# Biases of twelve projection tiles through TensorE, their copies on ScalarE, and newly written orders in a two-layer attention and expert kernel

## What is computed

```python
x = L0_attn_x
xn = _layernorm(x, axis=-1)
x = x + _L0_attn_ref(xn, ...) + _L0_ffn_ref(xn, ...)
xn = _layernorm(x, axis=-1)
x = x + _L1_attn_ref(xn, Wq, Wk, Wv) + _L1_ffn_ref(xn, Wg, W1, W2, W3)
```

```python
qg = x @ Wq + bq
Q, gate = (qg[..., :D], qg[..., D:])
K = x @ Wk + bk
V = x @ Wv + bv
...
scores = einsum('bhqd,bhkd->bhqk', rmsnorm(Q, qn_w), rmsnorm(K, kn_w)) / sqrt(HD)
out = einsum('bhqk,bhkd->bhqd', softmax(scores), V) * sigmoid(gate)[..., None]
return out @ Wo + bo
```

## Time and profile before

| | |
|---|---|
| median of 3 runs | 597.06 us (595.44 to 597.9) |
| the profiled execution | 595.26 us, of which the span of the instructions is 593.4 us |
| TensorE busy | 562.4 us (95%), weight loads 312.4 us (53%) |
| VectorE busy | 483.2 us (81%) |
| ScalarE busy | 416.4 us (70%) |
| GpSimd busy | 314.9 us (53%) |
| mean granted TensorE clock | 0.967 of full speed |

### The profile page before, as it was taken

One profiled execution on the slowest core, in us unless ns is written; L12 is line 12 of the kernel. 1 busy time (PEld: TensorE's weight loads), 2 busy tenths in 40 slices (PEclk: granted clock), 3 DMA queues, 4 the chain that ended last, 5 costly groups with the idle time before them and its releaser, 6 DMA issues.

```text
span 593.4 us, 11870 instructions
## 1 busy us (share of the span) xinstructions
PE 562.4 (95%) x3637; PEld 312.4 (53%) x3637; DVE 483.2 (81%) x1075; ACT 416.4 (70%) x824; POOL 314.9 (53%) x432
## 2 busy tenths in 40 slices
PE   7378999999999999999999999999999999999996
PEld 4243245456654555544747746576656557565431
DVE  7998889999989899997869988885774677888652
ACT  2542877986878789776875755668766767657795
POOL 6648754257836554677585443765176253233451
PEclk9865699999999999999999999999999999999999
DMA  8452443464644733466572644655645835633311
GB/s 267 129 213 62 134 128 108 129 191 140 194 148 139 210 116 107 137 198 211 158 223 95 218 125 148 195 156 191 189 147 178 261 111 163 195 93 81 91 50 36
DMA packets 68445, 90.01 MB, mean 152 GB/s; under 512 B 8480, under 2 KB 55328, under 8 KB 67872
## 3 DMA queue, kind: packets, MB, share of 16 engines
q1 hardware_dynamic: 64288, 80.87, 44.4%
q0 software_dynamic: 4096, 8.40, 4.8%
HBM read 66.04 MB, written 22.81 MB: 150 GB/s over the span
## 4 chain that ended last, share of the span: by engine, by line
PE 73%; DVE 13%; POOL 4%; issue 4%; ACT 3%; DMA 1%; POOLq 0%; DVEq 0%; ACTq 0%
PE slot L654 16%; PE slot L669 16%; PE pv_ps L682 16%; PE slot L631 9%; PE slot L644 7%; DVE mx L1107 5%; PE slot L619 2%; PE slot L611 2%; ACT probsT L827 2%; POOL xs_hbm L1201 1%; POOL yg L1212 1%; PE slot L576 1%; PE slot L690 1%; DMA yg<-ys_hbm,index 1%; PE slot L553 1%
## 5 line engine op out<-in xcount | busy, mean ns | idle before, releaser
L1107 DVE TENSOR_REDUCE mx<-slot 128x1 f32<-128x512 f32 x512 | 320.0, 681 | 59.7 <-PE slot L654 58.2
L827 ACT ACTIVATE probsT<-slot 128x512 f32<-128x512 f32 x512 | 272.3, 608 | 61.5 <-PE slot L669 49.3
L654 PE MATMUL slot<-k_stack,q_stack 72*128 72x512 bf16 x512 | 175.1, 395 | 3.0 <-DVE mx L1107 1.8
L669 PE MATMUL slot<-q_stack,k_stack 75*128 75x512 bf16 x512 | 167.0, 384 | 3.6 <-ACT probsT L827 1.3
L682 PE MATMUL pv_ps<-probsT,v 128*32 128x512 f32 x1024 | 118.1, 601 | 0.0
L1224 POOL TENSOR_TENSOR hid<-th,up 128x512 f32<-128x512 f32 (+2 forms) x56 | 71.1, 1274 | 78.4 <-DVE th L964 56.1
L654 PEld LDWEIGHTS slot<-k_stack,q_stack 72*128 72x128 bf16 x512 | 50.6, 100 | 80.0 <-issue 22.3
L669 PEld LDWEIGHTS slot<-q_stack,k_stack 75*128 75x128 bf16 x512 | 49.1, 98 | 66.9 <-issue 12.7
L1212 POOL DMA_INDIRECT yg<-ys_hbm,index x64 | 62.5, 977 | 33.0 <-DVE x L1000 15.8
L1201 POOL DMA_INDIRECT xs_hbm<-xn,index x64 | 64.0, 1000 | 26.4 <-issue 12.9
L631 PE MATMUL slot<-xgT,wbuf 128*128 128x128 f32 (+1 forms) x552 | 67.3, 276 | 0.0
(11 more groups left out here) (143 smaller groups left out, 538.5 us busy)
## 6 DMA issues: line engine op xcount, KB each, us to landing
wbuf<-in_experts SPq DMA_DIRECT2D x46, 544.0 KB, 4.8
q_stack<-parts_hbm SPq DMA_DIRECT2D x32, 288.0 KB
k_stack<-parts_hbm SPq DMA_DIRECT2D x96, 96.0 KB
wbuf<-in_experts SPq DMA_DIRECT2D x62, 128.0 KB, 2.2
xg<-xs_hbm SPq DMA_DIRECT2D x24, 256.0 KB, 3.5
ys_hbm<-ys SPq DMA_DIRECT2D x24, 256.0 KB, 3.8
parts_hbm<-parts SPq DMA_DIRECT2D x14, 384.0 KB
xs_hbm<-probsT SPq DMA_DIRECT2D x2, 2048.0 KB, 8.9
```

The source lines that it names most:

```text
L654: nc.tensor.matmul(ps[:, 0:N], q_stack[0:STACK, h, j * P:(j + 1) * P], k_stack[0:STACK, h, :], start=True, stop=True).then_inc(slot_full, 1)
L669: nc.tensor.matmul(ps[:, 0:N], k_stack[0:STACK + MAXROWS, h, j * P:(j + 1) * P], q_stack[:, h, :], start=True, stop=True).then_inc(slot_fu ...
L827: nc.scalar.activation(probsT[:, k % PROBS, a, :], ps[:, 0:N], ACT.Exp, scale=SCALE).then_inc(slot_free, 1)
L1107: nc.vector.tensor_reduce(mx[:, g, u // J, u % J:u % J + 1], ps[:, 0:N], AXIS.X, ALU.max)\
```

## The change

Three things are changed. For QV of the sequences 1 to 3 PE runs a second product into the same bank, the identity with `bias_tok`, which adds the bias there; ACT, not DVE, then copies the 256 and the 160 columns out. For sequence 0 all stays as it was. MP of the first group, MP(0, 0), is run by DVE. And the orders of all five engines and the banks are new, up to a place where layer 1 begins: from the 515th of 1320 stages on, PE's order is the same as before, and the other engines' orders join the old ones near the same place (ACT's with 489 stages to go, DVE's with 389, POOL's with 113, SP's with 119).

The beginnings of the orders, old (-) and new (+):

```diff
     "PE": """
-XT QV4 SU SG QK2 XT QV4 SG RK SD SU XT M2 QK M2 QK M7 QV M9 NT QV M3 QV M QV M XT E M E4 M2 E M E M E3 M2 E3 M
-E M4 E2 NT M2 PV E2 M E5 M SD M3 E3 QK E2 M2 E2 M2 E M QK M QV M E M QV M2 NT M4 PV M E M E2 M E2 M2 E XG M E
+XT QV4 SU SG XT QK2 QV4 SG SU RK M4 SD M QK M5 QK XT M10 QV NT QV3 M E M E M E2 M3 E XT E2 M3 E4 M E M E M E
+M2 E SD E M3 NT PV E M E3 M E M E QK M E2 M QK M3 QV M E M2 E2 M E M QV M E M E M2 NT E M3 E M PV M E3 M E M2
...
     "ACT": """
-XN XT SH2 XN HI2 XT MI2 SG GS RT SG SU XN SS SU QK HI QK XT HI NT XN XT E14 NT E GS E SS E12 QK E2 QK HI E GS
+XN XT SH2 XN XT HI2 MI SU MI SG QV4 SG RT SS XN SU QK GS QK XT HI QV GS HI NT XN QV2 E2 QV E4 XT E9 NT E SS E8
...
     "DVE": """
-CZ LN XV CS LN QQ QV QQ QV QQ SJ QQ SJ3 NH2 LN QV RE QV RE PT HAND PT QV4 RT GA RW GA SS SL SD NM LN M16 SW QV
-M2 QV M2 QV M12 QV M6 SS M NM M5 SD M2 GS M5 QV2 GS M GS M15 AT M2 QV2 M RT GA M3 SS M GA M6 RW M2 NM GA SL GA
+CZ LN CS XV LN QQ4 QV SJ4 NH QV NH QV LN RE QV RE PT2 HAND GA RT GA RW SS SL NM M16 LN MP SW SD M17 SS SD M4
+NM M5 GS M7 GS2 M23 AT GA M8 RT M SS GA M6 RW M3 GA SL GA NM M6 HAND GA M2 AT M GA M7 SW M2 GA M GA M6 OY M5 SD
...
     "POOL": """
-LN SX4 LN VS SQ BO LN GA SC3 BO SC LN MP PT2 SC BO2 MP SQ SC GA SC2 MP PT MP PT SQ GA MP GA3 SC3 GA MP GA SC
+LN SX4 LN BO VS SQ BO GA LN SC3 PT GA LN SC PT SQ MP SC BO SC3 BO MP2 PT2 SQ MP GA4 SC3 GA MP SC GA SC2 GA SC
...
     "SP": """
-ZERO PW RF2 ZERO WL3 NT RF WL RF WL3 NT PW WL3 RF WL XL WL NT WL XL WL2 XL WL2 NT XL WL XL RF WL6 YS NT RF XL
+ZERO PW RF2 WL ZERO RF WL3 NT WL3 RF WL2 NT PW WL3 RF XL NT XL WL3 RF XL WL NT WL6 XL2 WL2 NT RF WL YS XL PW
...
-PART_OF = {("DVE", "PT"): slice(0, 2), ("POOL", "PT"): slice(2, None), ("DVE", "SS"): slice(1, None),
-           ("ACT", "SS"): slice(1, None), ("DVE", "NM"): slice(1, None), ("ACT", "QK"): slice(2, None)}
+PART_OF = {("DVE", "MP"): slice(0, 1), ("POOL", "MP"): slice(1, None), ("DVE", "PT"): slice(0, 2), ("POOL", "PT"): slice(2, None), ("DVE", "SS"): slice(1, None),
+           ("DVE", "QV"): slice(0, J), ("ACT", "QV"): slice(J, None), ("ACT", "SS"): slice(1, None), ("DVE", "NM"): slice(1, None), ("ACT", "QK"): slice(2, None)}
```

The stages themselves:

```diff
@@ -550,8 +550,11 @@
                     pe.wait_ge(*emptied(("XT", A)))
                     if A == 0 and j == 0:
                         pe.wait_ge(first_in, 48)
-                    nc.tensor.matmul(ps[:, 0:2 * D + VGW[0]], xnT[:, A % 2, j * P:(j + 1) * P], w_tok[:],
-                                     start=True, stop=True).then_inc(slot_full, 1)
+                    last = nc.tensor.matmul(ps[:, 0:2 * D + VGW[0]], xnT[:, A % 2, j * P:(j + 1) * P], w_tok[:],
+                                            start=True, stop=(A == 0))
+                    if A >= 1:
+                        last = nc.tensor.matmul(ps[:, 0:2 * D + VGW[0]], ident[:], bias_tok[:], start=False, stop=True)
+                    last.then_inc(slot_full, 1)
                 elif kind == "VG":
                     A, half = stage[1:]
                     pe.wait_ge(*emptied(("XT", A)))
@@ -726,6 +729,12 @@
                     A = stage[1]
                     sc.wait_ge(*filled(stage))
                     nc.scalar.activation(xnT[:, A % 2, :], ps[:, 0:N], ACT.Copy).then_inc(slot_free, 1)
+                elif kind == "QV":
+                    A, j = stage[1:]
+                    sc.wait_ge(*filled(stage))
+                    nc.scalar.activation(qk_tok[:, 2 * j * D:2 * (j + 1) * D], ps[:, 0:2 * D], ACT.Copy)
+                    nc.scalar.activation(vgl[:, J * seq(A) + j, :], ps[:, 2 * D:2 * D + VGW[0]], ACT.Copy)\
+                        .then_inc(slot_free, 1)
                 elif kind == "QK":
                     A, a = stage[1:]
                     sc.wait_ge(*filled(stage))
@@ -896,12 +905,7 @@
                                             bias_tok[:, 0:2 * D], ALU.add).then_inc(qq_done, 1)
                 elif kind == "QV":
                     A, j = stage[1:]
-                    if A == 0:
-                        ve.wait_ge(qq_done, j + 1)
-                    else:
-                        ve.wait_ge(*filled(stage))
-                        nc.vector.tensor_tensor(qk_tok[:, 2 * j * D:2 * (j + 1) * D], ps[:, 0:2 * D],
-                                                bias_tok[:, 0:2 * D], ALU.add)
+                    ve.wait_ge(qq_done, j + 1)
                     nc.vector.tensor_tensor(vgl[:, J * seq(A) + j, :], ps[:, 2 * D:2 * D + VGW[0]],
                                             bias_tok[:, 2 * D:2 * D + VGW[0]], ALU.add).then_inc(slot_free, 1)
                 elif kind == "VG":
@@ -1106,6 +1110,16 @@
                     ve.wait_ge(*filled(stage))
                     nc.vector.tensor_reduce(mx[:, g, u // J, u % J:u % J + 1], ps[:, 0:N], AXIS.X, ALU.max)\
                         .then_inc(slot_free, 1)
+                elif kind == "MP":
+                    A, g = stage[1:]
+                    for u in range(HG * J):
+                        ve.wait_ge(*emptied(("M", A, g, u)))
+                    hi, mid, lo = (mx_parts[:, g, a] for a in range(MAXROWS))
+                    link(nc.vector.tensor_scalar(mx_neg[:], mx[:, g], -1.0, None, ALU.mult))
+                    link(nc.vector.tensor_copy(hi, mx_neg[:]))
+                    link(nc.vector.tensor_tensor(mx_rest[:], mx_neg[:], hi, ALU.subtract))
+                    link(nc.vector.tensor_copy(mid, mx_rest[:]))
+                    nc.vector.tensor_tensor(lo, mx_rest[:], mid, ALU.subtract).then_inc(mxp_done, 1)
                 elif kind == "AT":
                     A, f = stage[1:]
                     ve.wait_ge(*filled(stage))
```

More of the change, by code:

```diff
@@ new lines @@
+SG M RK E2 M DN E M GU E XG E PV E2 M2 E GU E M2 E QK E M XG M SG E QK M E AT E M SU XG DN M E M2 OT M E2 M2
+E2 M GU E NT M3 GU M PV E5 M XG M2 DN M E2 M OY E M2 E2 M DN M2 SD M E2 M NT M2 E M E GU E M3 DN M XG E SD E
+M2 E M E2 M GU M2 E M2 PV E M E2 M2 NT E DN M3 E2 M XG M E DN E M3 E M E M GU E M3 E M E PV E M E NT M2 E2 M E
+M E M E DN M E2 M2 E2 XG M E M2 GU E M2 E XG M E M E M AT E2 GU E2 M E PV M E M2 E M DN XG M E NT XG E M E M3
+E2 AT M E GU E PV E M2 E2 OT M DN M E2 M E2 M OY M2 E XT E M E3 M3 E QK M E M NT E GU M E VG M PV E VG E M E M
@@ new lines @@
+DN E M DN M2 E AT NT XT E QK E3 M2 VG2 M E XG M E2 M E GU M E2 M2 E M PV E M E2 RK XG E M E2 QK E M GU E M3 E
+QK M DN M E2 XG M2 NT E M2 E M DN M E2 M4 GU M2 E PV M E M E M E2 NT E M E M E M2 DN E M E2 M E2 M AT M2 E3 M
+E PV E M E M2 E2 M OT M E2 M E2 M NT OY M E3 M E2 M E2 M E PV M E3 M2 XG M E M E M E2 GG E UU E GG E NT GG E M
+UU M UU E M E M E M AT E M2 E DN E2 XG M E4 PV M XT M E3 M3 E3 M QK E M E2 M E M2 PV GG AT NT UU M GG2 UU2 M2
+OT E2 M2 OY DN M E2 M E M E2 M VG M2 E M QK M XT VG M E M2 E3 VG E M XG M E2 M NT VG M2 E M4 GG2 UU GG UU2 PV
@@ new lines @@
+QK GS QK HI QV E4 QV E2 NT E2 PO E6 XG2 HI E QV NT E6 GU E QV E5 XG E GU E2 RT SS E3 SU NT E DN E2 SG E3 DN E
+GU XG E3 PO E3 GU XG E QK E3 QK SG SU GS XG E DN OT E4 NT E GU2 E4 HI DN E3 XG E3 DN E NT E3 GU E DN E XG E4
+GU E HI E PO E NT E DN E4 XG DN E4 GU E3 NT E8 DN XG E5 XG E GU E3 GU E4 PO E DN XG E NT E4 GU E2 XN E2 XG OT
+DN E6 XT E6 NT E2 QK GU PO E XN E DN E DN E2 XT NT E3 QK HI E XG E4 RT E GU E HI E5 XG E2 QK E GU E QK E DN E
+XG NT E3 DN E2 GU E PO E3 NT E8 DN E9 OT E2 NT E13 XG E3 GG E PO E3 UU GG E UU GG UU NT E5 HI E DN E2 XG E2 XN
@@ new lines @@
+E XT E9 HI E PO QK NT GG UU GG UU GG UU OT E2 HI DN E4 XN QK E XT E8 NT XG E GG2 UU2 RT HI UU GG DN E10 QK E4
+XG E NT E GG UU3 E GG E GG E3 HI E2 PO DN E2 NT E XG E4 QK E5 UU GG E GG E UU GG UU NT E4 DN E11 XG PO E2 NT
+GG UU GG UU GG UU E6 DN E12 NT E XG E GG HI E UU GG UU E GG UU E5 DN E6 NT E6 XG E3 GG PO E GG UU2 E GG UU E
+DN E2 NT E11 XG E4 GG PO UU GG UU GG UU E5 DN NT E4 XG E9 XG GG E UU2 NT E GG2 UU E6 DN E12 NT E3 GG E UU PO
+GG E2 GG UU2 E7 DN E5 XG E2 UU GG2 NT E UU E GG UU PO E5 DN E NT E10 NT E19 NT E6 PO E23 PO
@@ L136 @@
+YG2 LN YG2 PT MP PT GA3 LN MP PT GA3 PT MP GA2 MP GA SC5 MP SC GA3 PT MP SC2 GA3 MP GA3 YG MP YG PT YG GA3 YG
+MP YG GA3 MP YG2 MP GA3 MP YG GA3 MP GA MP GA2 MP YG4 MP YG4
 """,
     "SP": """
[L138 to L140 removed]
@@ L144 @@
+WL2 NT XL RF WL2 XL WL2 NT PW RF WL4 NT YS2 RF2 WL2 NT XL WL PW WL RF WL NT WL XL YS RF WL YS NT WL4 NT RF XL
+YS WL3 XL NT YS XL RF WL3 NT RF YS XL WL2 RF WL NT WL PW WL2 XL WL NT WL RF YS WL RF NT WL4 RF NT OUT XL YS
+WL2 RF YS2 NT RF YS NT OUT NT2 OUT2
 """,
```

88 lines of the change are left out of this document (32 added, 56 removed).

## The result

The changed kernel takes 594.29 us (median of 12 runs, 593.05 to 602.71); the kernel before takes 598.40 us (median of 12, beside them on the same chip). The ratio is 0.9937 with an interval of [0.9913, 0.9961]: 0.6% faster. The profiled execution takes 593.87 us with a span of 592.1 us, against 595.26 us and 593.4 us before. The two profiles differ by 1.4 us, the medians by 4.1 us: the profiled run of before is one of its fastest.

A forecast was written before the change was run, and what follows sets the result against it. TensorE was taken to bound from 113 to 242 us, VectorE from 76 to 113, start-up waits before. Gains of 0.9 and 0.2 us sum to 1.1: profiled 595.26 becomes 594.2, median 596.0, own range 594 to 599.

The forecast's parts named there:

- likeliest case: Start-up waits at mask, NT and first E reappear, shifted by under 1 us; gain and products cancel; chance 0.43.
- second rival: TensorE's clock at its upper level from 50 us on: 4.7 us beyond the sum, 591.3 us; chance 0.17.
- step 7: Behind the first Exp: E(0,1,0,0) at 74.7 us instead of 75.6, 0.9 gained; 71 at full clock, 77.5 at half.
- Step 1: At the start, XT(1) before QK(0) moves the first HI from 17.26 to about 18.8 us, without effect yet.
- Step 2: Router's mask: four QV copies on ScalarE end at 25.8 us, router 1.65 us late, mask at about 31.8.
- Step 3: Between mask and first maximum VectorE loses 2.6 us of work: first maximum at about 39.0 us.
- Step 4: Sixteen maxima end near 48.6 us, then LN(3) 1.4 and MP 1.2: NT(0,0) at 51.4 us instead of 51.81.
- Step 5: Three QV(2) stages between NT and first E, 4.2 us at full clock, 8.4 at half: first E at 58.8, 0.9 later.
- Step 6: First Exp on ScalarE: no table load just ahead, Tanh's table loaded near 41 us; 59.2 us, 0.8 earlier.
- Step 8: From E(0,1,0,0) to where orders meet: +2.3 us of work, 2.5 given back by VectorE, net 0.2 us gained.
- first rival: VectorE bounds throughout and covers TensorE's added products: its 5.6 us are all gained, 591.5 us; chance 0.17.
- slower rival: Products paid, nothing returned: 5.6 us added, 602.7 us, decided if E(0,1,0,0) starts after about 77 us; chance 0.23.

The follow-up runs named there:

- e6: The changed kernel with only the first maxima's parts moved back to GpSimd: 594.03 us, ratio 0.9918.
- e5: The kernel before with products on zeros added where TensorE waits, 16 ahead of the first maxima's transpose and 8 ahead of the third E: 595.92 us, ratio 0.9959.
- e11: The kernel before, unchanged, profiled a second time: a run of 596.34 us, span 594.5 us.
- e1: The changed kernel without the added bias product of sequences 1 to 3, all orders kept: 595.10 us, ratio 0.9927.
- e10: The kernel before with products on zeros ahead of the first maxima's transpose, the third E and two E near 73 us: 592.75 us, ratio 0.9923.
- e12: The changed kernel with products on zeros added at 52, 237 and 286 us and at two places at 346 us: 592.91 us, ratio 0.9917.
- e2: The kernel before, orders unchanged, with the added bias product and VectorE copying where it added: 608.99 us, ratio 1.0188.
- e4: The changed kernel with sequence 1 back on VectorE's adds, without its product, and the maxima's parts ahead of the layer norm: 595.00 us, ratio 0.9950.
- e7: The changed kernel with one sum over gathered rows put two maxima and two gate products later on VectorE: 596.70 us, ratio 0.9967.
- e9: The changed kernel, orders kept, with products on zeros added at 52, 237 and 286 us: 594.79 us, ratio 0.9959.

## Why the prediction was right and wrong, step by step

The size was near, by luck: 596.0 us was forecast and 594.29 measured, at the lower edge of the forecast's own range of 594 to 599, but the gain was put at 1.1 us and is 4.1 between the medians. The forecast started from a median of 597.06 us for the kernel before, which is 598.40 beside the changed kernel. That the two profiles differ by 1.4 us, close to 1.1, is luck too: a lead of 4.7 us came and most of it went.

The likeliest case (start-up waits that reappear, products paid and returned) was not what happened. The mechanism was the second rival, the clock, to which I gave 0.17: it put the gain at 4.7 us beyond my sum, and step 7 had E(0,1,0,0) at 71 us for a clock that is full throughout. That start was 70.91 us; of the lead, 3 us were given back at 291 us in the profiled run. The forecast's own sign of being wrong came true as well: the clock between 40 and 76 us was not as before.

- **Step 1** held (18.83 us against 18.8). **Step 2** was mis-sized: the last copy ended at 26.99 us, not 25.8, and the router started 2.8 us late instead of 1.65. The table load ahead of the Tanh began at 22.14 us, 1.47 us later than before instead of 1.2. The copies themselves took 0.38 and 0.30 us, a little under the estimate; the last of them waited 0.82 us for TensorE, whose first pair of QV products ran at half clock. I had priced the engine that copies and not the one that fills the bank.
- **Step 3** followed from it: first maximum at 40.01 us, not 39.0. **Step 4**: layer norm 1.7 us and 0.4 us of idle time instead of 1.4, parts 1.04 instead of 1.2; with step 3's error the transpose was at 52.84 us, not 51.4. That the norm takes back what the move of the parts gains was right: e6, with the parts on GpSimd, has the transpose at 51.6 us and the same time.
- **Step 5** failed for a good reason: three QV of 1.40 us stand behind the transpose as said, but at full clock from 52.5 us on, and QV(2,0) with its two products now fills the wait ahead of the transpose (2.63 us idle before, 0.58 now). First E 57.45 us instead of 58.8. **Step 6** held: no table load ahead of the first Exp, the load at 42.06 us.
- **Step 7** is the step that failed: E(0,1,0,0) at 74.7 us was forecast with the clock of before, and against the clock rival I had held that the clock fell again in the M and E that follow, "and those stay as they were". They did stay; the clock did not. PV(0,0) took 3.6 us, not 4.99, and e5 and e11 show that the old orders do this way in 13.5 and 13.6 us too when the clock is granted.
- **Step 8** failed in both terms. The +2.3 us for the products: e1 shows 0.3 to 0.6 us for all twelve. The 2.5 us returned by VectorE: M(1,1,0) did come 12 us early, but PV(0,3) only 3.9 us, and at full clock (e10 against e12) the lead that VectorE's relief leaves is 1.1 us at PV(0,3), -0.4 us at PV(2,0) and nothing at the end. The step's result, E(2,3,1,1) at 240.9 us, was 239.29; but the way there took 168.4 us where 166.2 were forecast, and e1 takes 168.3 us without the products. What takes those 2 us is not shown.

The first rival (VectorE the bound throughout) held in its first half and fell by its second: e1 makes the products about 0.5 us of 8.4, but e10 keeps VectorE's adds and has the same time as the changed kernel. The rule that I weighed (the Trainium skill, Perfetto Trace Analysis, Identifying the Most-Contended Engine) takes the engine with the highest occupancy as the one to optimize first. On TensorE's room for the products the trace agrees with it (0.5 us of 8.4 in e1); on a gain from relieving VectorE it does not (e10).

The slower rival fell by its own condition: E(0,1,0,0) would have had to start after 77 us. e2 looks like that rival come true, in the old orders and with VectorE still copying: 83.3 us and 1.9% slower.

What stays open. The clock is granted run by run. Of the runs of before, the 47 with a mean clock from 0.957 to 0.9655 have a median of 598.6 us, the 28 above that 596.6 us. So the 4.1 us between the medians fit a clock that the changed kernel gets more often where it matters. That is argued from the means, which are a weak witness: the runs of e1 have a median mean clock of 0.967 and take as long as the changed kernel. Of before's runs at the median no profile was taken, so where a typical run has its half clock was not seen. Nor is it settled which of the new orders raises the clock: that QV with two products fill the wait ahead of the transpose is one candidate, yet e1, without them, is as fast.

The new orders also have a place of their own where the clock can fall. In the changed kernel, e1, e4, e6 and e7 TensorE waits 1.1 us for the mask of round 2 (here the changed kernel):

```profile
237.37 0.19 PE L604 MATMUL slot<-mask,lower_b 128*128 128x72 bf16 x1 [1.14 <-DVE mask L1063]
```

The changed kernel's profile kept its clock behind this wait. The other four were at half for 3.4 us from 238.6 to 240.9 us on, and from E(2,3,1,1) to PV(3,1) they took 35.6 to 35.8 us instead of 34.3. In the old orders (before, e5, e10, e11) TensorE's longest wait from 228 to 246 us is 0.55 us, and the clock of none fell.

## What to carry to other kernels

When a stretch gets faster and none of its own instructions changed, look at the granted clock before the orders: here 10 us at half clock behind the first E cost 4 us, and the change's whole gain was matched within the intervals by the old kernel with 34 products on zeros in TensorE's waits (ratio 0.9923 against 0.9937). Profile the kernel before twice when the effect is under 1%: its two profiles differed in the same places as the two kernels did. And follow a lead until it is gone: 1.2 us of order work vanished at one gather that ended at 306.9 us.

## What the runs showed of the hardware that was not expected

- The clock falls in different places in runs of one program: the kernel before had half clock from 63.3 to 73.5 us in one profile and not in the other, and from 293.7 to 297.1 us in the second alone.
- Waits and falls went together near 290 us in these profiles, with one exception. TensorE's longest wait between 284 and 298 us was 1.23, 1.66, 1.78 and 2.77 us in e5, the changed kernel, e11 and e7, and all four had a stretch of half clock from 291 to 299 us; it was 0.32 to 0.89 us in the first profile of before, e4, e6 and e10, was filled in e9 and e12, and none of these had one. But e1 waited 1.65 us and kept its clock. Near 237 us the same 1.1 us of waiting was followed by a fall in four profiles and not in a fifth.
- 24 products took 3.62 us in the changed kernel, where the clock was at half for the first 1.7 us of them (from 293.24 to 294.9 us), and 2.85 us at full clock in e12. One fall of 3.4 us cost about 1.6 us (7.65 against 6.02).
- Half clock ahead of 54 us cost little here: e10 runs at half from 40.8 to 54.5 us, has a mean clock of 0.974, and beats the changed kernel's profile at 0.980 by 1.9 us. The mean clock of a run said little; that of the stretch behind the first E said much.
- ScalarE's copies out of the banks took 0.38 us for 256 and 0.30 us for 160 columns of f32, where the 512-column Exp takes 0.61.
